# Gated cross-attention block on one core: head weights centred and scaled in place by GpSimd and split by ScalarE, ternary steps spread over three engines, factors and clip on GpSimd, one tile for v and vx

## The chip, the cores and the metric

The kernel runs on one core of one Trainium2 chip. The metric is device time in microseconds (us) from start to end of the execution; lower is better. TensorE (PE), VectorE (DVE), ScalarE (ACT) and GpSimd (POOL) each work through their own queue of instructions in order; SyncE (SP) issues the transfers, also in order. They wait for one another through semaphores.

## The reference, cut to what matters

```python
# x: 4 batches x 512 rows x 512; ctx: the same; 8 groups of heads, 2 query heads each, D = 128
ln  = layernorm(layernorm(x)) * ln_w + ln_b
q, k, v = (e4m3(clip(bf16(ln / in_scale), -448, 448)) * in_scale @ W.T * w_scale for each)
q, k = head_layernorm(q), head_layernorm(k)          # mean and variance over the 128 of a head
core = softmax(q @ k.T / sqrt(D)) @ v
qx   = head_layernorm(fp8_linear(ln, wqx));  kx, vx = split(ctx @ w_kv_x.T)
xout = softmax(qx @ head_layernorm(kx).T / sqrt(D)) @ vx
catq = e4m3(bf16(clip(concat(core, xout) / smooth, -448, 448)))
x    = x + tanh(g0) * (catq @ wproj.T) * proj_scale
# feed-forward: weights are made ternary: clip(round(w / mean|w|), -1, 1); activations 8 bit
x    = x + tanh(g1) * bitlinear(silu(a) * b, w_down),  a, b = split(bitlinear(layernorm(x), w_gate_up))
```

## The kernel before, in words

The attention part runs 32 iterations, one for each of the 4 batches and 8 groups of heads. An iteration has 16 slots, so there are 512 slots of scores, with 28 lead-in slots before the first and 20 after the last. Each engine's program is one loop over the slot number `n`, in which fixed tables say what else is to be issued in a slot (`PREP_HI`, `KV_AT`, `OUT_AT`, `X_AT`, `JOB_AT`); so the order of work on each engine is written out by hand. In every slot VectorE takes the row maximum of the scores (`row_max`), the reciprocal of the sums (`recip`) and the low half of the probabilities (`lo`); ScalarE takes the exponential and the high half; SyncE transposes the probabilities (`turn`); TensorE multiplies them with v some slots later. Numbers that need more than 16 bits are kept as a high and a low float16 half, and both are multiplied.

Work around that stream:

- **Head weights** (`prep_at`, `kv_at`), group by group during the lead-in and iterations 0 to 5, for later batches they are read back from `ws`. Two buffers `raw` take a quarter `kt` of a group's weights (128x768) or the context weights (128x1024). `head_means` (VectorE) takes the mean over each head, `center` (GpSimd) subtracts it, `prep_w` on GpSimd scales four column ranges into the high half, and `prep_w` on VectorE makes four low halves from them. `kv_hi` and `kv_lo` do the same for the context weights. `load_raw` refills a buffer after `w_dn`.
- **Heads**: `stats_a/b` (VectorE) and `rstd_a/b` (GpSimd) in even slots, `norm_a/b` and `v_lo` (VectorE) in odd ones, then transposes by TensorE, `head_y` (ScalarE), `head_hi` and `head_lo` (GpSimd).
- **group_factors** (VectorE), once for each iteration: five small instructions, one after another.
- **Outputs**: for each of two pairs in an iteration `out_step` (VectorE) clips, takes the exponent field, scales it and adds it, and `out_sub` (GpSimd) subtracts.
- **Jobs** (`JOBS`, `job`): from slot 92 to slot 305, 48 sums of the feed-forward weights (ScalarE) and 32 splits of the projection weights (GpSimd, VectorE, ScalarE); from slot 309 to 436, 48 ternary conversions (VectorE). They use the same two `raw` buffers, some six jobs in an iteration.

After the attention part comes the feed-forward part, 16 tiles of 128 rows. The change leaves it alone.

## Time and profile before

| | |
|---|---|
| median of three runs | 2029.97 us (2029.39 to 2035.35) |
| the profiled execution | 2037.14 us |
| its span in the trace | 2035.4 us |
| lead-in, up to the first row maximum | 0 to 138.06 us |
| iterations 0 to 5 | 138.06 to 507.78 us, 61.6 us each |
| iterations 6 to 18 | 507.78 to 1089.16 us, 44.7 us each |
| iterations 19 to 27 | 1089.16 to 1520.29 us, 47.9 us each |
| iterations 28 to 31 and feed-forward | 1520.29 to 2035.4 us |

An iteration's start is the start of its first row maximum on VectorE. Busy time is the time in which an engine executes an instruction; a row of a group gives the operation, the tile written and those read, partitions x elements, the count, busy us and mean ns, and then the engine's idle time just ahead and what ended it.

### The profile page before, as it was taken

The numbers are of one execution on the slowest core, as the hardware profiler recorded it, in microseconds if no ns is written. First come the engines' busy times: TensorE is split into PE (matmuls) and PEld (weight loads), VectorE is DVE, ScalarE is ACT, GpSimd is POOL, SyncE is SP. The second block draws the span as 40 slices with busy tenths as digits, with TensorE's granted clock in tenths as the row PEclk, the third lists the DMA queues.
The fourth block names the chain that finished last, engine by engine and source line by source line (L and its number), as shares of the span: only waits on it lengthen the run. The fifth ranks groups of instructions, "written<-read, shape, count | busy, mean of one in ns | idle before, by whom it ended". The sixth has DMA issues, their size and how long they took to land.

```text
span 2035.4 us, 34986 instructions
## 1 busy us (share of the span) xinstructions
PE 1677.8 (82%) x11147; PEld 1020.8 (50%) x11164; DVE 1747.3 (86%) x4062; ACT 1186.9 (58%) x2963; POOL 1017.2 (50%) x1327
## 2 busy tenths in 40 slices
PE   1467777767999988889998878898999967999996
...
GB/s 85 90 115 143 145 158 137 143 148 166 190 215 197 224 206 202 177 188 214 201 200 187 176 163 181 194 214 212 204 182 154 126 231 225 117 74 103 73 17 16
DMA packets 632027, 325.45 MB, mean 160 GB/s; under 512 B 547744, under 2 KB 590880, under 8 KB 626720
## 3 DMA queue, kind: packets, MB, share of 16 engines
q1 hardware_dynamic: 631840, 323.16, 67.6%
...
## 4 chain that ended last, share of the span: by engine, by line
DVE 44%; PE 28%; DMA 12%; POOL 7%; issue 7%; ACT 2%; SPq 1%; POOLq 0%; DVEq 0%; ACTq 0%
DVE pp L943 8%; DMA pt<-pp 8%; DVE nmx L933 8%; PE psum L682 5%; PE psum L640 4%; PE psum L657 4%; PE psum L628 4%; PE psum L600 4%; PE psum L699 3%; PE psum L607 3%; DMA raw<-in_w 3%; DVE xh L916 2%; DVE wbt L821 2%; POOL raw L1348 2%; DVE ast L902 1%
## 5 line engine op out<-in xcount | busy, mean ns | idle before, releaser
L628 PE MATMUL psum<-qk 128*128 128x512 f16 x1536 | 429.8, 390 | 71.4 <-DVE pp L943 69.3
L600 PE MATMUL psum<-wbt,xqt 128*128 128x256 f16 (+1 forms) x4096 | 421.6, 255 | 50.8 <-DVE xh L916 35.3
L600 PEld LDWEIGHTS psum<-wbt,xqt 128*128 128x128 f16 x4096 | 340.7, 102 | 167.3 <-DVE xh L916 40.1
L1231 ACT ACTIVATE psum<-psum,nmx 128x512 f32<-128x512 f32 x512 | 340.6, 665 | 143.7 <-DVE nmx L933 138.6
L943 DVE SCALAR_TENSOR_TENSOR pp<-psum,prs,pp 128x512 f16<-128x512 f32 x512 | 378.2, 739 | 31.0 <-ACT pp L1242 31.0
L1242 ACT ACTIVATE pp<-psum,prs 128x512 f16<-128x512 f32 x512 | 350.7, 685 | 62.5 <-DMA pt<-pp 62.4
L933 DVE TENSOR_REDUCE nmx<-psum 128x1 f32<-128x512 f32 x512 | 343.4, 671 | 26.9 <-PE psum L628 26.0
L1237 ACT ACTIVATE prs<-psm 128x1 f32<-128x1 f32 x512 | 107.4, 210 | 250.4 <-DVE psm L938 248.5
L640 PE MATMUL psum<-pt,vs 128*128 128x512 f16 x768 | 208.5, 396 | 52.7 <-ACT cy L1250 28.2
L1424 POOL TENSOR_TENSOR qk<-y,qk 128x512 f16<-128x512 f32 x192 | 233.3, 1215 | 16.0
L628 PEld LDWEIGHTS psum<-qk 128*128 128x128 f16 x1536 | 144.3, 100 | 162.7 <-DVE pp L943 74.0
L640 PE MATMUL psum<-pt,vx 128*128 128x512 f16 x768 | 203.6, 389 | 21.4 <-ACT cy L1250 19.6
L607 PE MATMUL psum<-wbt,ctxh 128*128 128x256 f16 x1536 | 199.8, 283 | 1.6 <-DVE ctxh L788 1.5
L1399 POOL TENSOR_TENSOR ars<-ast,eps 128x4 f32<-128x4 f32 x128 | 54.5, 426 | 286.8 <-DVE ast L903 286.7
L607 PEld LDWEIGHTS psum<-wbt,ctxh 128*128 128x128 f16 x1536 | 156.0, 102 | 54.7 <-issue 5.8
L1431 POOL TENSOR_TENSOR cy<-cy,cc 128x512 f16<-128x512 bf16 x128 | 152.6, 1193 | 41.2 <-DVE cy L959 41.2
L617 PE MATMUL psum<-idf,xh 128*128 128x128 f32 x768 | 121.0, 281 | 53.5 <-DVE vx L893 31.8
L1410 POOL TENSOR_TENSOR brs<-bst,eps 128x2 f32<-128x2 f32 x128 | 45.6, 356 | 236.7 <-DVE bst L910 236.1
L1224 ACT ACTIVATE y<-psum,hb,hw 128x512 f32<-128x512 f32 x192 | 151.3, 788 | 8.6 <-PE psum L617 8.6
L640 PEld LDWEIGHTS psum<-pt,vs 128*128 128x128 f16 x768 | 74.3, 100 | 159.4 <-issue 70.2
L1402 POOL TENSOR_TENSOR ars<-ars,mhalf 128x4 f32<-128x4 f32 x128 | 135.8, 1061 | 10.0
L1483 POOL TENSOR_SCALAR frs<-fmv 128x1 f32<-128x1 f32 x16 | 3.0, 191 | 267.4 <-DVE fmv L1013 267.3
...
## 6 DMA issues: line engine op xcount, KB each, us to landing
...
pt<-pp SPq DMA_TRANSPOSE x512, 3.3
...
```

The lines of the kernel that those rows point to most:

```text
L600: ins = e.matmul(bank[:, o0:o0 + c1 - c0], xv[:, v, kt * 512 + tt * 128:kt * 512 + (tt + 1) * 128], wb[i][:, h, kt, c0:c1], start=kt == 0 ...
L607: ins = e.matmul(bank[:, 256:512], ctxh[:, u, kt, ts], wkvb[i][:, w, kt, :], start=kt == 0 and k == 0, stop=kt == 3 and k == 2)
L628: ins = e.matmul(SB(n), qk[i][:, jq, u, ss], qk[i][:, jk, w, :], start=k == 0, stop=k == 2)
L640: ins = e.matmul(OB, v[:, t, u, :], src[:, w, t, :], start=t == 0 and k == 0, stop=t == 3 and k == 2)
L933: e.tensor_reduce(nmx[:, n % 8:n % 8 + 1], SB(n), AX, ALU.max, negate=True).then_inc(s["mx"], 1)
L943: e.scalar_tensor_tensor(pp[k][:, 1, :], SB(n), prs[:, n % 8:n % 8 + 1], pp[k][:, 0, :], ALU.mult, ALU.subtract).then_inc(s["lo"], 1)
L1224: e.activation(y32[n % 2][:], psum[:, BANK["T", n], :], ACT.Identity, bias=hb[:, vec:vec + 1], scale=hw[:, vec:vec + 1]).then_inc(s["y32"], 1)
L1231: e.activation(SB(n), SB(n), ACT.Exp, bias=nmx[:, k], accum_out=psm[:, k]).then_inc(s["exp"], 1)
L1242: e.activation(pp[n % 4][:, 0, :], SB(n), ACT.Copy, scale=prs[:, n % 8:n % 8 + 1]).then_inc(s["hi"], 1)
L1402: e.tensor_tensor(rs[:, 1, :], rs[:, 0, :], mhalf[:, 0:4], ALU.pow).then_inc(s["a_rs"], 1)
L1424: e.tensor_tensor(qk[it % 2][:, j, 1, :], y32[n % 2][:], qk[it % 2][:, j, 0, :], ALU.subtract).then_inc(s["hd_lo"], 1)
L1431: e.tensor_tensor(y.bitcast(F16), y, tmp, ALU.subtract).then_inc(s["o_q"], 1)
```

## The change

1. **Head weights.** GpSimd's `prep_scale` centres and scales each head in place in `raw` by one instruction with two factors (five of 128x128, and a sixth for v without a mean). ScalarE's `prep_hi` copies the 128x768 into the high half, VectorE's `prep_lo` makes the low half by one subtraction. `kv_scale`, `kv_hi`, `kv_lo` are the same for the context weights. The slots of the steps move (`PREP_AT`, `KV_AT`); the chain has one more engine in it.
2. **Ternary.** GpSimd scales and takes the lower of it and 1, VectorE takes the higher of it and -1 and adds the rounding constant, ScalarE takes it off again and writes bfloat16. Each is one slot after the other.
3. **Splits.** The subtraction moves from VectorE to GpSimd.
4. **group_factors and the clip** of the outputs move to GpSimd; the later steps of an output move back by one slot, its store too.
5. **v and vx** get one scale and one tile `vv`: one instruction of 128x256 in `v_hi` and in `v_lo` instead of two of 128x128.
6. `load_raw` of the next group's second quarter is issued ahead of `store_w` instead of behind it; in the lead-in two `head_means` stand earlier.

```diff
-PREP_HI = (-10, -6, -4, -1)
-KV_AT = {"part": 2, "spread": 3, "whole": 4, "fac": 5, "hi": 5, "lo": 6}
-OUT_AT = {"clip": 17, "field": 18, "step": 19, "add": 20, "sub": (21, 23), "store": 26}
+PREP_AT = (-9, -5, -3, 1)
+KV_AT = {"part": 2, "spread": 3, "whole": 4, "fac": 5, "scaled": 5, "hi": 6, "lo": 7}
+OUT_AT = {"clip": 17, "field": 19, "step": 20, "add": 21, "sub": (22, 24), "store": 27}
...
-            def prep_w(it, kt):
+            def prep_lo(it, kt):
                 k, i = it * 5 + kt, it % 2
-                r = raw[k % 2]
-                for c0, c1, v in COLS:
-                    q.wait_ge("w_hi", (it * 4 + kt) * 4 + v + 1)
-                    ins = e.scalar_tensor_tensor(wb[i][:, 1, kt, c0:c1], r[:, c0:c1], ratio[:, v, kt:kt + 1],
-                                                 wb[i][:, 0, kt, c0:c1], ALU.mult, ALU.subtract)
-                ins.then_inc(s["w_dn"], 1)
+                q.wait_ge("w_hi", it * 4 + kt + 1)
+                e.tensor_tensor(wb[i][:, 1, kt, :], raw[k % 2][:, 0:768], wb[i][:, 0, kt, :],
+                                ALU.subtract).then_inc(s["w_dn"], 1)
...
+            def ternary(m):
+                if JOBS[m][0] == "tern":
+                    f = raw[(K0 + m) % 2][:, 0:512]
+                    q.wait_ge("l_t0", JV["l_t2", m])
+                    e.tensor_scalar(f, f, -1.0, MAGIC, ALU.max, ALU.add).then_inc(s["l_t1"], 1)
...
+            def prep_hi(it, kt):
+                k, i = it * 5 + kt, it % 2
+                q.wait_ge("wc", it * 4 + kt + 1)
+                q.wait_ge("gb", (it - 1) * 4)
+                q.wait_ge(f"w_st{i}", 16 * (it // 2))
+                e.activation(wb[i][:, 0, kt, :], raw[k % 2][:, 0:768], ACT.Copy).then_inc(s["w_hi"], 1)
...
+            def prep_scale(it, kt):
+
+                k = it * 5 + kt
                 r = raw[k % 2]
+                q.wait_ge("wm", k + 1)
                 q.wait_ge("const_ready", 1)
+                for h, (c, v) in enumerate(HEAD_COLS):
+                    e.tensor_scalar(r[:, c:c + 128], r[:, c:c + 128], wmean[:, k % 2, h:h + 1], ratio[:, v, kt:kt + 1],
+                                    ALU.subtract, ALU.mult)
...
+            def out_clip(pair):
+                y = cy[pair % 3][:]
+                q.wait_ge("o_y", 2 * pair + 2)
+                e.tensor_scalar(y, y, 448.0, -448.0, ALU.min, ALU.max).then_inc(s["o_c"], 1)
```

On VectorE, in an iteration that prepares weights, a quarter's low half stood as four instructions behind the output step, directly ahead of the next quarter's means:

```order
L957 TENSOR_SCALAR cc<-cc 128x1024
L821 SCALAR_TENSOR_TENSOR wbt<-raw,ratio,wbt 128x256 x2
L821 SCALAR_TENSOR_TENSOR wbt<-raw,ratio,wbt 128x128 x2
L813 TENSOR_REDUCE wmean<-raw 128x5
L814 TENSOR_SCALAR wmean<-wmean 128x5
```

After the change, the same place for the first quarter of a group; `wmean` now belongs to a slot of its own:

```order
L896 TENSOR_TENSOR xh<-psum,ars 128x512
L804 TENSOR_TENSOR wbt<-raw,wbt 128x768
L918 RECIPROCAL psm<-psm 128x1
L913 TENSOR_REDUCE nmx<-psum 128x1
L923 SCALAR_TENSOR_TENSOR pp<-psum,prs,pp 128x512
L890 BN_STATS bst<-psum 128x6
L798 TENSOR_REDUCE wmean<-raw 128x5
```

Four instructions became one, and the low half is two slots behind the scaling instead of one.

On GpSimd before, one quarter between the output subtraction and the next `rstd_a`:

```order
L1348 TENSOR_TENSOR raw<-raw,wmean 128x640
L1367 TENSOR_SCALAR wbt<-raw,ratio 128x256 x2
L1367 TENSOR_SCALAR wbt<-raw,ratio 128x128 x2
L1399 TENSOR_TENSOR ars<-ast,eps_0 128x4
L1402 TENSOR_TENSOR ars<-ars,mhalf 128x4
```

and after, in the fullest slot, where a head, the clip and a quarter stand behind one another ahead of the next `rstd_b`:

```order
L1416 TENSOR_TENSOR qk<-y_1,qk 128x512
L1447 TENSOR_SCALAR cy<-cy 128x1024
L1355 TENSOR_SCALAR raw<-raw,wmean,ratio 128x128 x5
L1357 TENSOR_SCALAR raw<-raw,ratio 128x128
L1402 TENSOR_TENSOR brs<-bst,eps_1 128x2
L1404 TENSOR_TENSOR brs<-brs,mhalf 128x2
```

Five instructions of a quarter became six, and the clip stands ahead of them. On SyncE before, the refill of `raw` behind the store of a whole group (`ws`):

```order
L395 DMA_TRANSPOSE pt<-pp 128x8x128 x6
L383 DMA ws<-wbt 128x8192
L379 DMA raw<-in_w 128x768
L395 DMA_TRANSPOSE pt<-pp 128x8x128
L379 DMA raw<-in_w 128x768
```

and after:

```order
L377 DMA raw<-in_w 128x768
L393 DMA_TRANSPOSE pt<-pp 128x8x128
L381 DMA ws<-wbt 128x8192
L393 DMA_TRANSPOSE pt<-pp 128x8x128
L377 DMA raw<-in_w 128x768
```

The first refill moved ahead of the store, with one transpose between them.

## Rows read from the trace of the kernel before

**Rows 1.** The page, part 1: busy time, share, instructions.

```profile
PE 1677.8 (82%) x11147; PEld 1020.8 (50%) x11164; DVE 1747.3 (86%) x4062; ACT 1186.9 (58%) x2963; POOL 1017.2 (50%) x1327
```

**Rows 2.** Windows: the stages of the kernel, busy us by engine.

```profile
core 0: us, PE busy (x) PEld busy (x) DVE busy (x) ACT busy (x) POOL busy (x), PEclk, DMA share, GB/s
0.00:138.06 138.06, 48.65 (x312) 35.96 (x313) 90.76 (x235) 17.51 (x33) 68.71 (x110) 0.74 0.27 93
138.06:507.78 369.72, 272.10 (x1785) 171.59 (x1784) 323.16 (x753) 202.62 (x506) 237.43 (x320) 0.90 0.63 148
507.78:1089.16 581.38, 531.03 (x3880) 348.45 (x3878) 553.02 (x1281) 465.63 (x1247) 374.92 (x472) 0.99 0.89 201
1089.16:1520.29 431.13, 373.92 (x2675) 238.90 (x2673) 414.08 (x1006) 293.03 (x749) 239.22 (x294) 0.98 0.85 190
1520.29:2035.40 515.11, 452.10 (x2504) 225.92 (x2519) 366.26 (x795) 208.12 (x430) 96.94 (x135) 0.95 0.46 114
```

**Rows 3.** Windows, columns as before: iterations 29, 9, 8 and 20.

```profile
1563.28:1602.42 39.14, 39.14 (x298) 26.53 (x297) 37.02 (x89) 31.09 (x81) 23.89 (x32) 1.00 0.62 122
641.68:682.80 41.12, 38.93 (x292) 25.71 (x291) 39.55 (x94) 36.07 (x98) 27.23 (x35) 1.00 0.89 207
596.31:641.68 45.37, 41.52 (x311) 27.51 (x309) 43.31 (x103) 35.08 (x95) 31.13 (x43) 1.00 1.02 224
1139.76:1193.38 53.62, 42.38 (x303) 26.25 (x301) 53.10 (x131) 32.55 (x82) 27.01 (x32) 1.00 0.80 175
```

**Rows 4.** Groups by form: the head weights on VectorE and GpSimd.

```profile
L821 DVE SCALAR_TENSOR_TENSOR wbt<-raw,ratio,wbt 128x256 f16<-128x256 f32 x64 | 37.8, 629 | 35.2 <-POOL wbt L1367 35.2
L821 DVE SCALAR_TENSOR_TENSOR wbt<-raw,ratio,wbt 128x128 f16<-128x128 f32 x64 | 28.0, 475 | 0.0
L837 DVE SCALAR_TENSOR_TENSOR wbt<-raw,wfa,wbt 128x1024 f16<-128x1024 f32 x8 | 10.2, 1275 | 3.2 <-POOL wbt L1376 3.2
L1348 POOL TENSOR_TENSOR raw<-raw,wmean 128x640 f32<-128x640 f32 x32 | 40.9, 1277 | 16.2 <-DVE wmean L814 16.2
L1367 POOL TENSOR_SCALAR wbt<-raw,ratio 128x128 f16<-128x128 f32 x64 | 32.8, 523 | 0.0
L1367 POOL TENSOR_SCALAR wbt<-raw,ratio 128x256 f16<-128x256 f32 x64 | 30.0, 479 | 3.2
L1259 ACT ACTIVATE raw<-raw 128x512 f32<-128x512 f32 x48 | 31.1, 647 | 0.0
```

**Rows 5.** Waits: VectorE for a refill of `raw`.

```profile
DVE wmean L813 <- DMA raw<-in_w: 7.5, 6, 2.8
```

**Rows 6.** Groups by form: clip, split, ternary, v on VectorE.

```profile
L952 DVE TENSOR_SCALAR cy<-cy 128x1024 bf16<-128x1024 bf16 x64 | 30.7, 480 | 11.9 <-ACT cy L1250 11.9
L984 DVE TENSOR_TENSOR raw<-raw,wps 128x512 f16<-128x512 f32 x32 | 30.2, 943 | 0.0
L976 DVE TENSOR_SCALAR raw<-raw,wsc 128x512 f32<-128x512 f32 x48 | 23.9, 497 | 0.3 <-DMA raw<-in_wgu 0.3
L977 DVE TENSOR_SCALAR raw<-raw 128x512 bf16<-128x512 f32 x48 | 21.1, 439 | 1.6
L978 DVE TENSOR_SCALAR raw<-raw 128x512 bf16<-128x512 bf16 x48 | 15.8, 329 | 1.7
```

**Rows 7.** Windows of the instructions that touch `kfac`: VectorE, then ScalarE.

```profile
0.00:2035.40 2035.40, 52.47 (x160) 45.01 (x64) 0.94 0.68 160
```

**Rows 8.** Groups by form: long elementwise work on GpSimd.

```profile
L1376 POOL TENSOR_SCALAR wbt<-raw,wfa 128x1024 f16<-128x1024 f32 x8 | 8.9, 1118 | 0.8
L1424 POOL TENSOR_TENSOR qk<-y,qk 128x512 f16<-128x512 f32 x192 | 233.3, 1215 | 16.0
L1418 POOL TENSOR_SCALAR qk<-y 128x512 f16<-128x512 f32 x192 | 119.3, 621 | 32.6 <-ACT y L1224 31.0
```

**Rows 9.** Source lines on VectorE: ns min/median/max, first and last start.

```profile
L957 DVE TENSOR_SCALAR cc<-cc x64: 407/976/1332, 210.5 to 1701.3; 128x1024 bf16<-128x1024 bf16 x64
L955 DVE TENSOR_SCALAR cc<-cy x64: 398/408/819, 206.2 to 1700.9; 128x1024 uint16<-128x1024 uint16 x64
```

More of the change, by code:

```diff
@@ L288, in flamingo @@
         qk = [a(f"qk{i}", [128, 6, 2, 512], F16) for i in range(2)]
-        vs = [a(f"vs{i}", [128, 4, 2, 128], F16) for i in range(3)]
-        vx = [a(f"vx{i}", [128, 4, 2, 128], F16) for i in range(3)]
+        vv = [a(f"vv{i}", [128, 4, 2, 2, 128], F16) for i in range(3)]
         pp = [a(f"pp{i}", [128, 2, 512], F16) for i in range(4)]
@@ L637, in pv @@
                     q.wait_ge("o_y", hc)
-                src, v = pt[hc % 2], vx[it % 3] if att else vs[it % 3]
+                src, v = pt[hc % 2], vv[it % 3]
                 for k, (u, w) in enumerate(((0, 0), (0, 1), (1, 0))):
-                    ins = e.matmul(OB, v[:, t, u, :], src[:, w, t, :], start=t == 0 and k == 0, stop=t == 3 and k == 2)
+                    ins = e.matmul(OB, v[:, t, u, att, :], src[:, w, t, :], start=t == 0 and k == 0, stop=t == 3 and k == 2)
                 if t == 3:
@@ L1078, in dve_program @@
             ins.then_inc(s["pre_h"], 1)
+            head_means(0, 0)
+            head_means(0, 1)
             for t in range(4):
@@ L1099, in dve_program @@
             e.tensor_tensor(hr2[:, 2:4], hf[:, 2:4], hm2[:, 0:2], ALU.mult).then_inc(s["pre_r"], 1)
-            for kt in range(4):
-                head_means(0, kt)
-                prep_w(0, kt)
+            prep_lo(0, 0)
+            head_means(0, 2)
+            prep_lo(0, 1)
+            head_means(0, 3)
             for col, v in ((0, 0), (1, 0), (2, 1), (3, 1), (4, 2)):
@@ L1144, in dve_program @@
                         stats_b(it, tt)
-                for k, step in enumerate(("clip", "field", "step", "add")):
+                for k, step in enumerate(("field", "step", "add")):
                     for pair in pairs_at(n, OUT_AT[step]):
                         out_step(pair, k)
-                for it, kt in prep_at(n - 1):
-                    prep_w(it, kt)
+                for it, kt in prep_at(n - 2):
+                    prep_lo(it, kt)
                 for it, kt in prep_at(n + 1):
@@ L1259, in job @@
                     e.activation(f, f, ACT.Abs, accum_out=wsum[:, col:col + 1]).then_inc(s["l_sum"], 1)
+                elif what == "tern":
+                    q.wait_ge("l_t1", JV["l_t2", m])
+                    q.wait_ge(f"l_st{i}", JV[f"l_st{i}", JB[m][0]])
+                    e.activation(o.bitcast(BF16)[:, 0:512], f, ACT.Identity, bias=magic[:, 0:1]).then_inc(s["l_t2"], 1)
                 elif what == "split":
@@ L1268, in act_program @@
                     x_turned(0, kt, v)
+                prep_hi(0, v)
+            kv_hi(0)
             q.wait_ge("pre_w", 1)
@@ L1283, in act_program @@
                     head_y(it, o)
+                for it, kt in prep_at(n - 1):
+                    prep_hi(it, kt)
+                for it in kv_at(n, "hi"):
+                    kv_hi(it)
                 for b, kt in x_steps(n, "turn"):
@@ L1446, in pool_program @@
             for kt in range(4):
-                prep_w(0, kt)
+                prep_scale(0, kt)
             w_spread(0)
             c_spread(0)
-            kv_hi(0)
+            kv_scale(0)
             for kt in range(4):
                 ctx_hi(0, kt)
+            group_factors(0)
             for n in range(FIRST, PAST):
+                ph, j = divmod(n, SLOTS)
+                if j == FACTORS_AT and 0 < ph + 2 < NIT:
+                    group_factors(ph + 2)
                 for it, tt, half in tiles_at(n - 1):
@@ L1461, in pool_program @@
                     head_lo(it, o)
+                for pair in pairs_at(n, OUT_AT["clip"]):
+                    out_clip(pair)
                 for k in range(2):
@@ L1465, in pool_program @@
                 for it, kt in prep_at(n):
-                    prep_w(it, kt)
+                    prep_scale(it, kt)
                 for it in kv_at(n, "spread"):
                     w_spread(it)
-                for it in kv_at(n, "hi"):
-                    kv_hi(it)
+                for it in kv_at(n, "scaled"):
+                    kv_scale(it)
                 for b, _ in x_steps(n, "rstd"):
```

166 lines of the change are left out of this document (71 added, 95 removed).

## Prediction

> **What bounds the kernel now.** I read the page's busy shares first: VectorE is busy 86% of the span, TensorE 82%, ScalarE 58%, GpSimd 50% [rows 1]. That is a mean over stages with different limits, so the windows by stage come next; the reader should compare, in each, busy VectorE and busy TensorE with the length [rows 2].
>
> - Iterations 0 to 5: 369.7 us, VectorE 323.2 (87%), TensorE 272.1 (74%, at a granted clock of 0.90), GpSimd 237.4. TensorE has room; VectorE and what it waits for set the pace. By the groups its idle time is largely a wait for GpSimd's scaled weights: 35.2 us ahead of the low halves over the whole kernel [rows 4], and 7.5 us ahead of the means, for a refill of `raw` [rows 5].
> - Iterations 6 to 18: 581.4 us, VectorE 553.0 (95%), TensorE 531.0 (91%). Iterations 19 to 27: 431.1 us, VectorE 414.1 (96%), TensorE 373.9. VectorE is the fuller one, but another limit stands close by: iteration 29, without weights and jobs, takes 39.14 us, and TensorE is busy in all of them at full clock; iteration 9 with jobs takes 41.12; iteration 8 takes 45.37 with the transfer engines busy for all of it (share 1.02) [rows 3]. So 39.1 us is TensorE's floor for an iteration, and some iterations are held by transfers.
> - The rest, 515 us, holds four short iterations and the feed-forward part, where the change has almost nothing.
>
> **The sum, part by part.** It is made against the profiled execution's own 2037.1 us (span 2035.4); the median of the three runs is 7.2 us lower, and I carry that over at the end.
>
> *Head weights.* VectorE spends 37.8 + 28.0 busy and 35.2 waiting on 32 quarters, 3.16 us each [rows 4]. A 128x768 subtraction with two inputs is not in the trace. From below, the 128x512 of the split at 0.94 [rows 6], from above the 128x1024 low half at 1.28 [rows 4]; midway, 1.1. That is 2.05 us less for each quarter, if ScalarE's copy is ready two slots after the scaling. Eleven of the quarters lie in the lead-in, 21 in iterations 0 to 5. GpSimd did 1.28 + 2 x 0.52 + 2 x 0.48 = 3.3 us for a quarter [rows 4]; its six 128x128 instructions are 3.1 at that row's 0.52 (the two-factor form isn't shown; it could cost 4.0 if each were half as long again). ScalarE gets a copy of 128x768: 0.65 for 512 [rows 4], so 0.97, and it has 45% of its time free there [rows 2]. The context weights change by nothing much: one low half of 1.28 stays one.
>
> *Refill.* It stood behind a 2 MB store, now ahead of it, and every refill has two slots: the 7.5 us [rows 5] go, nearly all in iterations 0 to 5. If the slots shrink too far, they stay.
>
> *Clip and factors.* VectorE loses 30.7 us of clips [rows 6] and 52.5 us of instructions on `kfac` [rows 7], together 83.2, or 2.6 us in each of 32 iterations. GpSimd gets two clips of 128x1024, 1.12 each by its nearest row [rows 8], and four tiny ones; 3 us an iteration. The joined v instruction I count as nothing: two neighbours of 128x128 overlap.
>
> *Splits.* 30.2 us leave VectorE [rows 6], all in iterations 6 to 18; GpSimd's subtraction of that size takes 1.2 [rows 8], 32 times 39 us on a GpSimd that is busy 374.9 of 581.4.
>
> *Ternary.* Three instructions, 60.8 us and 3.6 between them [rows 6], become one like the first, 23.9: 40.5 us off VectorE. GpSimd and ScalarE each get 0.6 us six times an iteration [rows 4, 8]; they have room.
>
> Now by stage:
>
> 1. Lead-in: 11 x 2.05 = 23, and little else. VectorE waits there for GpSimd's `rstd` in any case, a refill takes longer than two short slots, and the first `head_means` now stand ahead of the x statistics. I keep 15.
> 2. Iterations 0 to 5: 21 x 2.05 = 43, 7.5 of refills, 6 x 2.6 = 16; 66 in all. The new chain passes through three in-order queues: while ScalarE waits for `prep_scale`, the next exponential is queued behind it, and VectorE's reciprocal waits for that. In the fullest slot GpSimd has a head (1.84), a clip (1.12) and a quarter (3.1) to do, 6 us where a slot is 3. I take 0.6 us for each of 21 quarters, 13 us. 66 - 13 = 53: 51 to 52 us for a plain iteration. If that chain fits, all 66 come; if each quarter waits 2 us, only 24.
> 3. Iterations 6 to 18: VectorE's 553.0 fall by 34 and 30 to 489, 37.6 an iteration, under TensorE's 39.1. From there TensorE and the transfers set the time: 39.1, the 2.0 by which iteration 9 exceeds it, and 1.7 for iterations that transfers hold (8, 16) or that also prepare the next x: 42.8, times 13 = 556. That is 25 less, not 64.
> 4. Iterations 19 to 27: VectorE's 414.1 fall by 23 and 40.5 to 350. Iteration 20 is the fullest, 53.62 with VectorE at 53.10 [rows 3]; it and its two neighbours come down by some 7 us each, the six others by 2.3 each until TensorE and transfers hold them near 42.5. That is 35.
> 5. Iterations 28 to 31: already at the floor; 1. Feed-forward: nothing.
>
> Sum: 15 + 53 + 25 + 35 + 1 = 129; 2037.1 - 129 = 1908 for such an execution, and 7 less for the median: **1901 us**.
>
> **A rule against it.** The row of the step instruction has a minimum of 407 ns and a median of 976, that of the exponent field, of the same size, a median of 408 [rows 9]: the same kind of work takes 0.57 us longer where it meets something, and that slot is the one in which GpSimd does a head.
> The Trainium skill (SBUF — State Buffer, Who interferes with whom) says that VectorE in a two-port mode or with two inputs from SBUF and GpSimd hold one shared pair of ports exclusively, so that whoever comes second stands still; the trace agrees with it in those two rows. By that rule more GpSimd work makes VectorE's remaining steps longer; by a reading without it the steps keep their mean.
> By the rule the sum is that of the first rival, 1946; by the rows with their mean unchanged it is 1901.
>
> **The rivals.**
>
> *VectorE and GpSimd get in each other's way.* GpSimd goes from 39.6 us an iteration to 43 of 52 (iterations 0 to 5), and from 28.8 to 35 of 42.8 (6 to 18): 29 + 2 clips 2.2 + factors 0.8 + 2.5 splits 3.0. Each iteration has six output steps on VectorE; two already pay 0.57. If the other four do as well, that is 2.3 us an iteration, 73 over 32; about 1 us of it an iteration hides in TensorE's lead in the later stages, so 45 remain: 1946. For it: the 0.57. Against: the field stood behind the statistics without a delay, and GpSimd pays when it comes second. Chance 0.15.
>
> *TensorE and transfers hold everything from iteration 6 on.* For it: iteration 29 at 100% TensorE, and the transfer share of 0.89 and 0.85 in both stages. Then only lead-in and iterations 0 to 5 gain, and 10 us of the rest: 2030 - 68 - 10 = 1952. Against: iterations 20 to 22 are 53 us with TensorE at 42. Chance 0.12.
>
> *All that leaves VectorE pays.* Lead-in 23, iterations 0 to 5 66, 6 to 18 down to 40.1 each, 60, iterations 19 to 27 50, 2 at the end: 201, 1829. It needs transfers to stretch no further and GpSimd never late. Chance 0.15.
>
> *Slower: GpSimd's queue delays `rstd`.* There are 256 `rstd`, each due one slot after its statistics, and VectorE stands still for a late one; behind it `norm`, and TensorE's bank behind that. New work ahead of them in the queue is 1.1 to 3 us at a time. It decides from 129 / 256 = 0.5 us of added delay for each; at 0.6 the time is 1901 + 154 = 2055. Against: `rstd` stands first in its slot, and GpSimd is not above 85% in any stage. Chance 0.05.
>
> **How the numbers follow.** My forecast (1875 to 1925) has 0.50; the rivals 0.15, 0.12, 0.15, 0.05, and 0.03 is left for mixtures beyond them. The bounds of single costs move it: new waits per quarter 0 to 2 us (+13 to -29), the 128x768 at 0.94 or 1.28 (5 us either way), two-factor instructions at 4.0 a quarter (some 10 us more). From 1848 to 1948 the range takes in the forecast, the first rival, half of the second and a third of the third. Within 0.3% (6 us) a measurement can't tell this kernel's time from no change: faster 0.94, same 0.01, slower 0.05.
>
> **What would show it in the profile after.** Iterations 0 to 5 at 50 to 53 us, no wait of VectorE on scaled weights, and the low half at 0.95 to 1.3 us; iterations 6 to 18 near 42.8 with VectorE's share below TensorE's; iterations 20 to 22 at 46 to 47; the first row maximum near 123 us. Wrong it is if the step, field and add rows on VectorE grow by half a microsecond (first rival), if VectorE waits for `ars` and `brs` come to over 100 us (the slower one), if stages after slot 96 don't move (second), or if GpSimd's clip costs twice 1.12.

## The result: 1.4% slower, and the profile after

| | us, median (lowest to highest) |
|---|---|
| before, timed beside the change | 2032.66 (2029.39 to 2036.19) |
| after | 2059.98 (2057.23 to 2066.28) |
| ratio | 1.0138, 95% interval 1.0107 to 1.017 |
| profiled execution of after | 2066.28, span 2064.5 |

Forecast were 1901 us and a range of 1848 to 1948. The page's part 1 of the kernel after, to set beside [rows 1]:

```profile
PE 1692.5 (82%) x11147; PEld 1028.2 (50%) x11164; DVE 1592.2 (77%) x3487; ACT 1228.9 (60%) x2923; POOL 1301.7 (63%) x1655
```

VectorE lost 155 us of work, TensorE did the same matmuls, and the time rose: what left VectorE was not paid back. GpSimd gained 284 us, more than left VectorE. Part 4 of the page, the chain that ended last, names the new pacemaker. First before, then after:

```profile
DVE 44%; PE 28%; DMA 12%; POOL 7%; issue 7%; ACT 2%; SPq 1%; POOLq 0%; DVEq 0%; ACTq 0%
...
POOL 35%; PE 27%; DVE 20%; DMA 8%; issue 5%; ACT 4%; SPq 1%; POOLq 0%; DVEq 0%; ACTq 0%
```

GpSimd's share went from 7% to 35%. The windows by stage, bounds by the same slots as [rows 2] (columns as there: lead-in's own row is left out):

```profile
145.32:511.33 366.01, 276.98 (x1770) 171.47 (x1769) 296.90 (x627) 219.87 (x509) 299.11 (x391) 0.87 0.63 151
511.33:1109.15 597.82, 540.63 (x3881) 354.36 (x3880) 505.72 (x1104) 459.55 (x1194) 435.07 (x579) 0.97 0.87 196
1109.15:1546.24 437.09, 374.99 (x2675) 240.42 (x2673) 350.91 (x809) 313.30 (x762) 358.64 (x398) 0.98 0.85 188
```

In the next table the first column is a length in us, the others are differences from it; e7 is the fastest of the experiments below.

| stage | before | forecast | after | best variant (e7) |
|---|---|---|---|---|
| lead-in | 138.1 | -15 | +7.3 | -4.5 |
| iterations 0 to 5 | 369.7 | -53 | -3.7 | -38.7 |
| 6 to 18 | 581.4 | -25 | +16.4 | +2.4 |
| 19 to 27 | 431.1 | -35 | +6.0 | -24.5 |
| rest | 515.1 | -1 | +3.2 | -3.6 |

VectorE is busy for 81%, 85% and 80% of the three stages; no engine is over 91% in any of them, so waits must hold the kernel. Groups by form of the kernel after show two surprises and two confirmations:

```profile
L1355 POOL TENSOR_SCALAR raw<-raw,wmean,ratio 128x128 f32<-128x128 f32 x160 | 135.4, 857 | 3.9 <-DVE wmean L799 3.8
L1433 POOL TENSOR_SCALAR raw<-raw,wsc 128x512 f32<-128x512 f32 x48 | 100.1, 2086 | 1.3 <-DMA raw<-in_wgu 0.4
L1447 POOL TENSOR_SCALAR cy<-cy 128x1024 bf16<-128x1024 bf16 x64 | 70.3, 1098 | 25.9 <-ACT cy L1228 20.5
L804 DVE TENSOR_TENSOR wbt<-raw,wbt 128x768 f16<-128x768 f32 x32 | 38.3, 1196 | 6.3 <-ACT wbt L1187 6.3
L896 DVE TENSOR_TENSOR xh<-psum,ars 128x512 f32<-128x512 f32 x128 | 87.5, 684 | 67.0 <-POOL ars L1394 66.1
L905 DVE TENSOR_TENSOR xh<-psum,brs 128x256 f32<-128x256 f32 x128 | 53.5, 418 | 68.0 <-POOL brs L1404 68.0
L944 DVE TENSOR_SCALAR raw<-raw 128x512 f32<-128x512 f32 x48 | 23.6, 493 | 57.4 <-POOL raw L1433 57.4
```

The clip (1098 ns against 1120) and the 128x768 low half (1.20 us against 1.1) cost what was forecast. Centring and scaling of 128x128 costs 857 ns where 520 were taken, a quarter 5 x 0.857 + 0.425 = 4.7 us instead of 3.1; the ternary's first step costs 2.09 us where 0.6 were taken, 48 times. Two waits of VectorE come with it: 57.4 us for GpSimd's step of the ternary conversion, and 66.1 + 68.0 = 134 us for the two `rstd`, 35.0 of it in the lead-in, 52.6 in iterations 0 to 5 and 35.0 in 6 to 18. Before, the two `rstd` cost 14.3 (who waited for whom, us in total, times, longest):

```profile
DVE xh L916 <- POOL ars L1402: 9.6, 9, 1.4
DVE xh L925 <- POOL brs L1412: 4.7, 8, 1.2
```

How such a wait comes about, in the timeline of GpSimd and VectorE in the kernel after, in iteration 17 (start, duration, engine; in brackets the idle time before):

```profile
1027.12 0.43 DVE L890 BATCH_NORM_STATS2 bst<-psum 128x6 f32<-128x256 f32 x1 [0.40 <-PE psum L606]
...
1027.67 1.04 POOL L1447 TENSOR_SCALAR cy<-cy 128x1024 bf16<-128x1024 bf16 x1
...
1028.79 0.62 POOL L1437 TENSOR_SCALAR wps<-raw 128x512 f16<-128x512 f32 x1
...
1029.49 1.16 POOL L1442 TENSOR_TENSOR raw<-raw,wps 128x512 f16<-128x512 f32 x1
...
1030.61 0.19 POOL L1402 TENSOR_TENSOR brs<-bst,eps 128x2 f32<-128x2 f32 x1
...
1030.88 0.71 POOL L1404 TENSOR_TENSOR brs<-brs,mhalf 128x2 f32<-128x2 f32 x1
...
1031.68 0.42 DVE L905 TENSOR_TENSOR xh<-psum,brs 128x256 f32<-128x256 f32 x1 [2.13 <-POOL brs L1404]
```

The statistics are ready at 1027.55. GpSimd takes them up at 1030.61, because the clip, the high half and the moved subtraction of the split (L1447, L1437, L1442) stand in front. VectorE stands for 2.13 us. That `rstd` is first in its slot doesn't help: the slot before is still being worked off.

### The profile page after: what moved, and what is told of

Same layout as the page of the kernel before. It is cut to its first block, busy times and chain, and to the rows that moved or that the text cites. A ratio compares the mean times of both kernels' runs of the same rounds, so it can differ in the third digit from the quotient of the medians.

```text
span 2064.5 us, 34605 instructions
## 1 busy us (share of the span) xinstructions
PE 1692.5 (82%) x11147; PEld 1028.2 (50%) x11164; DVE 1592.2 (77%) x3487; ACT 1228.9 (60%) x2923; POOL 1301.7 (63%) x1655
## 4 chain that ended last, share of the span: by engine, by line
POOL 35%; PE 27%; DVE 20%; DMA 8%; issue 5%; ACT 4%; SPq 1%; POOLq 0%; DVEq 0%; ACTq 0%
DMA pt<-pp 8%; POOL raw L1355 6%; PE psum L681 5%; POOL qk L1416 5%; PE psum L656 5%; DVE pp L923 4%; POOL raw L1433 4%; DVE nmx L913 4%; PE psum L639 4%; PE psum L627 3%; PE psum L599 3%; POOL cy L1423 3%; POOL brs L1404 3%; PE psum L698 3%; POOL ars L1394 3%
## 5 line engine op out<-in xcount | busy, mean ns | idle before, releaser
L627 PE MATMUL psum<-qk 128*128 128x512 f16 x1536 | 438.1, 396 | 47.2 <-DVE pp L923 46.4
L639 PE MATMUL psum<-pt,vv 128*128 128x512 f16 x1536 | 414.2, 394 | 70.6 <-ACT cy L1228 37.2
L599 PE MATMUL psum<-wbt,xqt 128*128 128x256 f16 (+1 forms) x4096 | 426.0, 256 | 49.7 <-DVE xh L896 34.6
L639 PEld LDWEIGHTS psum<-pt,vv 128*128 128x128 f16 x1536 | 151.2, 101 | 276.5 <-issue 98.2
L1416 POOL TENSOR_TENSOR qk<-y,qk 128x512 f16<-128x512 f32 x192 | 240.1, 1250 | 16.0
L606 PEld LDWEIGHTS psum<-wbt,ctxh 128*128 128x128 f16 x1536 | 154.1, 101 | 60.8 <-DVE ctxh L787 12.1
L1423 POOL TENSOR_TENSOR cy<-cy,cc 128x512 f16<-128x512 bf16 x128 | 147.6, 1154 | 19.4 <-DVE cy L937 19.4
L1394 POOL TENSOR_TENSOR ars<-ars,mhalf 128x4 f32<-128x4 f32 x128 | 134.9, 1054 | 10.0
L1410 POOL TENSOR_SCALAR qk<-y 128x512 f16<-128x512 f32 x192 | 125.9, 656 | 24.0 <-ACT y L1202 18.3
L896 DVE TENSOR_TENSOR xh<-psum,ars 128x512 f32<-128x512 f32 x128 | 87.5, 684 | 67.0 <-POOL ars L1394 66.1
L1355 POOL TENSOR_SCALAR raw<-raw,wmean,ratio 128x128 f32<-128x128 f32 x160 | 135.4, 857 | 3.9 <-DVE wmean L799 3.8
```

The lines of the kernel that those rows point to most:

```text
L599: ins = e.matmul(bank[:, o0:o0 + c1 - c0], xv[:, v, kt * 512 + tt * 128:kt * 512 + (tt + 1) * 128], wb[i][:, h, kt, c0:c1], start=kt == 0 ...
L606: ins = e.matmul(bank[:, 256:512], ctxh[:, u, kt, ts], wkvb[i][:, w, kt, :], start=kt == 0 and k == 0, stop=kt == 3 and k == 2)
L627: ins = e.matmul(SB(n), qk[i][:, jq, u, ss], qk[i][:, jk, w, :], start=k == 0, stop=k == 2)
L639: ins = e.matmul(OB, v[:, t, u, att, :], src[:, w, t, :], start=t == 0 and k == 0, stop=t == 3 and k == 2)
L1355: e.tensor_scalar(r[:, c:c + 128], r[:, c:c + 128], wmean[:, k % 2, h:h + 1], ratio[:, v, kt:kt + 1], ALU.subtract, ALU.mult)
L1394: e.tensor_tensor(rs[:, 1, :], rs[:, 0, :], mhalf[:, 0:4], ALU.pow).then_inc(s["a_rs"], 1)
```

## Experiments

The stages of each run, in us; bounds by the same slots. Ratios are to the kernel before, run beside it, with 95% intervals; "before" and "after" have their numbers in the section above.

| run | time, ratio | lead-in | 0 to 5 | 6 to 18 | 19 to 27 | rest |
|---|---|---|---|---|---|---|
| before | | 138.1 | 369.7 | 581.4 | 431.1 | 515.1 |
| after | 1.0138 | 145.3 | 366.0 | 597.8 | 437.1 | 518.3 |
| e1 | 2022.82, 0.993 [0.9908, 0.9952] | 134.9 | 333.1 | 600.1 | 437.7 | 516.5 |
| e2 | 2056.4, 1.0092 [1.0065, 1.012] | 146.3 | 366.0 | 600.3 | 427.0 | 517.3 |
| e3 | 2071.83, 1.0174 [1.0133, 1.0214] | 145.4 | 368.8 | 594.4 | 447.9 | 518.9 |
| e4 | 1995.82, 0.9778 [0.9733, 0.9823] | 134.8 | 333.9 | 600.1 | 412.4 | 511.8 |
| e5 | 1991.73, 0.9766 [0.9742, 0.9791] | 134.8 | 334.0 | 605.1 | 401.4 | 518.4 |
| e6 | 1983.0, 0.9736 [0.9713, 0.9759] | 134.3 | 332.8 | 597.2 | 402.4 | 512.9 |
| e7 | 1970.25, 0.9678 [0.9651, 0.9705] | 133.6 | 331.0 | 583.7 | 406.6 | 511.5 |
| e8 | 1973.38, 0.9688 [0.9652, 0.9725] | 134.6 | 333.6 | 591.0 | 404.6 | 515.8 |
| e9 | 1987.28, 0.9771 [0.9739, 0.9803] | 133.6 | 331.7 | 597.4 | 403.3 | 517.7 |
| e10 | 1976.15, 0.9705 [0.9667, 0.9743] | 133.0 | 341.8 | 578.8 | 411.8 | 515.7 |
| e11 | 2005.57, 0.9876 [0.9832, 0.992] | 137.9 | 358.2 | 577.7 | 416.1 | 507.0 |
| e12 | 2143.56, 1.0553 [1.0533, 1.0573] | 137.9 | 361.8 | 571.8 | 425.6 | 645.8 |
| e13 | 2096.67, 1.0321 [1.0301, 1.0341] | 138.0 | 352.2 | 550.0 | 409.7 | 645.5 |

The stages of a run are read from one profiled execution, and several executions of one kernel differ by up to 17 us. Where two kernels have the same code in a stage, it can be seen how well a length repeats: iterations 6 to 18 are the same in after, e1, e2 and e4, and took 597.8, 600.1, 600.3 and 600.1 us; iterations 19 to 27 are the same in e4 and e5, apart from one last split, and took 412.4 and 401.4. So a difference of 2 to 3 us between two stages means nothing in what follows, and in 19 to 27 one of ten can be chance.

### What does an instruction cost on GpSimd? (m1, a micro kernel)

GpSimd alone runs twelve forms of the same instruction, three times each, with no work on the other engines meanwhile.

> Twelve forms of GpSimd's tensor_scalar by themselves, 128x512 float32 (two of them 128x128), three times each, nothing beside them; x is only copied to the output, the rest of the computation is left out. Theory A (the pair of operations sets the price, whatever runs beside it): multiply by a pointer and multiply by 1.0 takes 0.6 us, multiply and minimum about 2.1, subtract and multiply about 2.4 to 2.8, subtract and multiply on 128x128 0.8. Theory B (the long times in the changed kernel come from VectorE at the shared ports): all forms of one size take 0.6 us here, those of 128x128 0.4.

The source lines of that kernel (ns minimum, median, maximum): L40 multiplies by a pointer operand and by 1.0; L41 multiplies by a pointer and takes a minimum; L42 is the same with immediates (numbers written in the instruction); L43 takes minimum and maximum by immediates, L44 both by pointer; L45 subtracts and multiplies by pointers, L46 by immediates; L47 multiplies twice by pointers; L48 multiplies and adds, L51 with immediates; L49 and L50 are L45 and L40 at 128x128.

```profile
L40 POOL TENSOR_SCALAR z<-t,p x3: 686/686/687, 3.4 to 32.1; 128x512 f32<-128x512 f32 x3
L41 POOL TENSOR_SCALAR z<-t,p x3: 2002/2002/2010, 4.2 to 32.9; 128x512 f32<-128x512 f32 x3
L42 POOL TENSOR_SCALAR z<-t x3: 1917/1917/1918, 6.3 to 35.0; 128x512 f32<-128x512 f32 x3
L43 POOL TENSOR_SCALAR z<-t x3: 612/612/613, 8.3 to 37.0; 128x512 f32<-128x512 f32 x3
L44 POOL TENSOR_SCALAR z<-t,p x3: 757/757/757, 9.0 to 37.7; 128x512 f32<-128x512 f32 x3
L45 POOL TENSOR_SCALAR z<-t,p x3: 2076/2076/2077, 9.9 to 38.6; 128x512 f32<-128x512 f32 x3
L46 POOL TENSOR_SCALAR z<-t x3: 1922/1922/1922, 12.1 to 40.8; 128x512 f32<-128x512 f32 x3
L47 POOL TENSOR_SCALAR z<-t,p x3: 767/767/767, 14.1 to 42.8; 128x512 f32<-128x512 f32 x3
L48 POOL TENSOR_SCALAR z<-t,p x3: 687/687/687, 14.9 to 43.7; 128x512 f32<-128x512 f32 x3
L49 POOL TENSOR_SCALAR z<-t,p x3: 792/792/792, 15.7 to 44.4; 128x128 f32<-128x128 f32 x3
L50 POOL TENSOR_SCALAR z<-t,p x3: 367/367/368, 16.6 to 45.3; 128x128 f32<-128x128 f32 x3
L51 POOL TENSOR_SCALAR z<-t x3: 617/617/617, 17.1 to 45.8; 128x512 f32<-128x512 f32 x3
```

Size, types and layout of the 128x512 forms are equal, and the cost is 0.61 to 0.77 us or 1.9 to 2.1 us. A pointer in place of an immediate costs 0.07 to 0.09, two of them 0.15. What decides is the pair of operations: multiply-multiply, multiply-add and minimum-maximum are cheap, multiply-minimum and subtract-multiply dear. Nothing ran beside it, so neighbours and ports are no part of that; in the kernel the two dear forms are another 8% and 4% longer (857 against 792 ns, 2086 against 2002). Subtract-multiply is a little cheaper here than the 2.4 to 2.8 that were expected.

### The cheap forms in the kernel (e1, e4), and the ternary back on VectorE (e2)

e1 replaces the five subtract-multiply pieces of a quarter, and the four of the context weights, by one centring and multiply-multiply pieces, in place:

```diff
-                for h, (c, v) in enumerate(HEAD_COLS):
-                    e.tensor_scalar(r[:, c:c + 128], r[:, c:c + 128], wmean[:, k % 2, h:h + 1], ratio[:, v, kt:kt + 1],
-                                    ALU.subtract, ALU.mult)
+                q.done(e.tensor_tensor(cols, cols, wmean[:, k % 2, 0:5].unsqueeze(2).broadcast_to([128, 5, 128]),
+                                       ALU.subtract))
+                for c0, c1, v in COLS:
+                    ins = e.tensor_scalar(r[:, c0:c1], r[:, c0:c1], ratio[:, v, kt:kt + 1], 1.0, ALU.mult, ALU.mult)
```

> The changed kernel, but the head weights are centred by one tensor_tensor and scaled by four instructions that multiply twice, in place, as the kernel before did them (3.3 us a quarter by its rows instead of 4.7). Theory A (the form of the six instructions costs the gain in iterations 0 to 5): these iterations come down from 61.0 us to 54 to 57, the first row maximum from 145 to 138 or less, the total by 25 to 45 us, to 2015 to 2035. Theory Q (the place in GpSimd's queue matters, not the form): less than 10 us.

e4 adds that the ternary clips before it scales: GpSimd takes minimum and maximum with the mean and its negative, VectorE multiplies by the reciprocal and adds the rounding constant.

```diff
-                    e.tensor_scalar(f, f, wsc[:, k:k + 1], 1.0, ALU.mult, ALU.min).then_inc(s["l_t0"], 1)
+                    e.tensor_scalar(f, f, wsc[:, k - 2:k - 1], wsc[:, k - 4:k - 3], ALU.min, ALU.max).then_inc(s["l_t0"], 1)
...
-                    e.tensor_scalar(f, f, -1.0, MAGIC, ALU.max, ALU.add).then_inc(s["l_t1"], 1)
+                    e.tensor_scalar(f, f, wsc[:, k:k + 1], MAGIC, ALU.mult, ALU.add).then_inc(s["l_t1"], 1)
```

> The changed kernel with all its work on the same engines, but in forms that were short by themselves: the head weights as in the earlier run (centre by one tensor_tensor, then multiply twice), and the ternary step as minimum and maximum against plus and minus the mean on GpSimd, multiply and add on VectorE, add on ScalarE. Theory A (the slow forms are all that went wrong): 1960 to 1990, iterations 23 to 26 at 43, iterations 6 to 18 below 581. Theory A+Q (forms cost stages 0 to 5 and 19 to 27, the queue costs 6 to 18): 2000 to 2015, with iterations 6 to 18 still at 595 to 600 and 23 to 26 at 43 to 44.5.

Groups of e4, the same work as L1355 and L1433 of after:

```profile
L1358 POOL TENSOR_TENSOR raw<-raw,wmean 128x640 f32<-128x640 f32 x32 | 42.9, 1340 | 12.0 <-DVE wmean L800 11.9
L1361 POOL TENSOR_SCALAR raw<-raw,ratio 128x256 f32<-128x256 f32 x64 | 35.8, 571 | 3.2
L1361 POOL TENSOR_SCALAR raw<-raw,ratio 128x128 f32<-128x128 f32 x64 | 24.6, 396 | 0.0
L1435 POOL TENSOR_SCALAR raw<-raw,wsc 128x512 f32<-128x512 f32 x48 | 40.0, 833 | 4.7 <-DMA raw<-in_wgu 3.8 <-DMA raw<-in_wd 0.8
```

A quarter falls to 1.34 + 2 x 0.57 + 2 x 0.40 = 3.3 us, near the 3.1 of the sum, and a ternary step to 0.83. Where these stand the time falls: e1 takes 10 us from the lead-in and 33 from iterations 0 to 5 and nothing elsewhere; e4 takes 25 more from 19 to 27. Together they turn +1.4% into -2.2%; from after to e4 the span is 71.5 us shorter. e1 came as theory A said. e4 came between its two theories (1995.82), with iterations 6 to 18 still at 600 as the second said.

e2 is after with the ternary's three steps on VectorE, as before.

> The changed kernel, but the ternary conversion is VectorE's alone again, three instructions as before. Theory A (GpSimd's multiply-and-minimum of 2.09 us makes VectorE stand, 57 us in all): iterations 23 to 26 come from 46.9 us to 44 to 45, the total falls by 10 to 20 us. If the three-engine version is worth having, the total rises instead by up to 20.

Iterations 23 to 26 fall from 46.9 to 43.6 us each and the stage by 10 to 427.0, less than by e4's 25. The whole fell by less than the 10 to 20 us expected: 1.0092 against 1.0138, with overlapping intervals. So moving the ternary off VectorE was probably worth it, but only in the cheap form.

### Who delays `rstd` in iterations 6 to 18? (e3, e5 to e10)

With cheap forms these iterations still take 600 us; nothing dear runs there. e3 is after with the clip one slot later: `OUT_AT = {"clip": 18, ...}` instead of 17.

> The changed kernel with one number changed: GpSimd's clip stands one slot later, in an even slot behind rstd, not in the odd slot behind a head. No work is added or taken away. Theory Q (rstd is late because head, clip and job stand ahead of it in GpSimd's queue): VectorE's waits for rstd in iterations 6 to 18 (35 us) fall by half or more and these iterations by 8 to 20 us in all, iterations 0 to 5 by 5 to 15. Theory A alone: no change in iterations 6 to 18.

The wait for `brs` fell from 68.0 to 37.9 over the kernel, but VectorE's exponent field, now close behind the clip, waited 66.2 us for it:

```profile
DVE cc L933 <- POOL cy L1447: 66.2, 49, 14.0
DVE xh L896 <- POOL ars L1394: 64.7, 30, 5.5
DVE xh L905 <- POOL brs L1404: 37.9, 26, 6.0
```

In iterations 6 to 18 the waits for `rstd` fell from 35.0 to 20.2 us, and the one for the clip put 25.1 in their place; the stage fell by 3.4 us where theory Q had 8 to 20, and iterations 0 to 5 didn't fall at all. The wait changed its name: a new place in the queue is not enough. The next runs take work off the queue, on top of e4: e5 returns the split's subtraction to VectorE, e6 the clip, e8 both, e9 the factors alone, e7 all three. Each moves back the lines of the diff for that part, for example for e6:

```diff
+                for pair in pairs_at(n, OUT_AT["clip"]):
+                    y = cy[pair % 3][:]
+                    q.wait_ge("o_y", 2 * pair + 2)
+                    e.tensor_scalar(y, y, 448.0, -448.0, ALU.min, ALU.max).then_inc(s["o_c"], 1)
```

> As e4, and the split's subtraction is VectorE's again. If GpSimd's queue costs iterations 6 to 18 (head, clip and split stand ahead of rstd in one slot), these fall by 8 to 20 us against e4, though VectorE gets 30 us more to do; if VectorE's load sets them, they rise by up to 20. No other stage moves.

> As e4, and the clip is VectorE's again, in the same slot. By the queue theory the waits for rstd fall in all stages and the total by 10 to 25 us; iterations 6 to 18 by 5 to 15. If VectorE's load sets the time, nothing or up to 10 us more.

> As e4, with split, clip and factors all on VectorE again; what stays of the change is the head weights by three engines, the ternary step by three engines, one tile for v and vx, the later output slots and the refill ahead of the store. By the queue theory iterations 6 to 18 come to 575 to 582 as in the kernel before and VectorE's wait for rstd to under 20 us; the total 1975 to 2000. If VectorE's load sets the time it is slower than e4 by 10 to 30.

> The changed kernel with the cheap head-weight and ternary forms, with the split's subtraction and the clip back on VectorE, and the factors of a group still on GpSimd. Its 6 to 18 were 597.8 us in the changed kernel, 605.1 with the split alone back, 597.2 with the clip alone back and 583.7 with split, clip and factors back. Theory A (GpSimd's queue ahead of rstd, and the two large pieces are what is long in it): with both gone the factors' four instructions (1.45 us an iteration) are too short to matter; its 6 to 18 are 583 to 588, VectorE's waits for rstd under 6 us in them, the time 1970 to 1976. Theory B (the factors in their slot are what meets rstd): its 6 to 18 stay at 594 or above, the waits for rstd stay above 8 us, the time is 1980 to 1990.

> The changed kernel with the cheap forms, and the factors of a group back on VectorE; split subtraction and clip stay on GpSimd. Theory A (split and clip make the queue long): its 6 to 18 stay at 594 to 602, the waits for rstd above 20 us, the time 1988 to 1998. Theory B (the factors are what meets rstd): its 6 to 18 fall to 583 to 590, the waits for rstd below 12 us, the time 1975 to 1985.

In iterations 6 to 18, waits of VectorE for `ars` and `brs` together, and the stage: after 35.0 and 597.8; e4 35.0 and 600.1; e5 8.5 and 605.1; e6 17.4 and 597.2; e9 27.9 and 597.4; e8 under 6 and 591.0; e7 about 1 and 583.7. Against e4 no single part brings more than 3 us, which is within the spread, the two large ones 9, all three 16.4. e9 came as its theory A said (its time 1 us under that range), and so did e8 but for the stage, 3 us over: split and clip together are what is long in the queue. e7 came as the queue theory said to within 2 us of its stage and of its waits, with a total 5 us under the range. That the factors add the last 7 us isn't shown: e7 and e8 differ by 0.1% in time (0.9678 and 0.9688), and e8's profiled execution was 8 us above its median. e5 and e6 missed what the queue theory forecast for this stage (8 to 20 and 5 to 15 us), and e6's total fell in 19 to 27 instead. The waits for `rstd` alone don't give the length either: e5 cuts them to a quarter and gains nothing, as VectorE has 15.6 us more work and waits 15.7 us for the split's high half. TensorE slows too: from before to after its busy time there grows from 531.0 to 540.6 us while its granted clock falls from 0.99 to 0.97 (0.95 to 0.97 in e1 to e6, e8 and e9), and in e7 both are back. Whether the lower clock lengthens the stage or only follows from TensorE's longer pauses, no run separates:

```profile
464.59:1048.33 583.74, 531.01 (x3889) 347.48 (x3887) 546.55 (x1227) 462.65 (x1195) 364.69 (x472) 0.99 0.88 201
```

e10 puts e7's output steps back into their old slots, each one earlier.

> As the kernel with cheap forms and split, clip and factors back on VectorE (its 6 to 18: 583.7 us, time 1970.3), and the steps of an output pair back in the slots that they had before the change (field 18, step 19, add 20, sub 21 and 23, store 26: each one earlier). Theory A (TensorE and the transfers hold its 6 to 18, and the slots of these steps are indifferent): its 6 to 18 are 581 to 586, the time 1966 to 1974. Theory B (the later slots of the steps cost what VectorE's shorter work should have given): its 6 to 18 fall to 572 to 579, the time is 1958 to 1966.

Stage 6 to 18 goes to 578.8, as theory B said, but iterations 0 to 5 to 341.8, 11 us longer, and the time, 1976.15, is in neither range; the two kernels' intervals overlap. The later slots cost nothing on balance.

### Why iterations 6 to 18 never gain (e11 to e13)

Even e7, with 6.5 us less work on VectorE, is no shorter there than before. So the last runs start from the kernel before. e11 relieves VectorE and loads nobody: clip, multiplication and addition of an output pair work on 8 of 1024 columns.

```diff
-                    ins = e.tensor_scalar(y, y, 448.0, -448.0, ALU.min, ALU.max)
+                    ins = e.tensor_scalar(y[:, 0:8], y[:, 0:8], 448.0, -448.0, ALU.min, ALU.max)
```

> The kernel before, with the clip, the multiplication and the addition of an output pair done on 8 of the 1024 columns, so the output lacks that rounding: VectorE is relieved of some 1.6 us a pair, two pairs an iteration, about 43 us in its 6 to 18 (26 pairs at 414, 847 and 670 ns, less some 60 to 100 ns each that a tiny one takes), and nothing is put on another engine. Theory A (beside VectorE, TensorE with its gaps and the transfers of the probabilities hold an iteration in its 6 to 18, so relief of VectorE could not have paid there whatever GpSimd did): its 6 to 18 fall by less than 10 us, to 571 or more, and the waits for the transfers of pt grow by 10 us or more. Theory B (VectorE, busy for 95% there, was the bound, and the changed kernel lost its relief to GpSimd's queue alone): its 6 to 18 fall by 25 to 43 us, to 538 to 556. As in the forecast (its 6 to 18 limited by TensorE's 39.1 us of busy time and some 3.7 of gaps): a fall of 20 to 27 us, to 554 to 561.

e12 thins transfers instead, e13 does both:

```diff
-                e.dma_start(wbt[:, it % 2, :], ws[it % NG]).then_inc(s[f"w_ld{it % 2}"], 16)
+                e.dma_start(wbt[:, it % 2, 0:2048], ws[it % NG][:, 0:2048]).then_inc(s[f"w_ld{it % 2}"], 16)
...
-                e.dma_start(raw[k % 2][:, 0:512], late_src[src][:, j, :]).then_inc(s[f"raw_ld{k % 2}"], 16)
+                e.dma_start(raw[k % 2][:, 0:128], late_src[src][:, j, 0:128]).then_inc(s[f"raw_ld{k % 2}"], 16)
```

> The kernel before with thinner transfers: from iteration 6 on an iteration loads a quarter of its weights (0.5 MB instead of 2 MB; the rest are the weights that the buffer held), and a job loads 128 of its 512 columns; the output is computed from those. No engine's work changes. The kernel before spends 581.4 us in its 6 to 18. Theory A (three limits lie within some 5 us an iteration: VectorE in iterations 12 to 14, TensorE and the transfers of the probabilities, queued behind the weights and the jobs, in the others): its 6 to 18 fall by 3 to 12 us, and the waits of TensorE and ScalarE for pt<-pp (19.2 and 18.5 us) fall below 20 together. Theory B (transfers don't limit): its 6 to 18 within 3 us of 581.

> As the kernel with the clip, multiplication and addition of an output pair on 8 columns (its 6 to 18: 577.7 us, the waits for pt<-pp 21.9 and 21.6), and the transfers thinned as well (a quarter of the weights from iteration 6 on, a quarter of each job's load). Theory A (the transfers are what held that kernel when VectorE was relieved): its 6 to 18 fall to 550 to 568, near the 13 x 42.8 = 556 of the forecast or below, with TensorE busy for 94% or more and the waits for pt<-pp under 20 us together. Theory B (something else than VectorE and transfers holds them: TensorE itself, its clock, ScalarE): its 6 to 18 stay at 573 or more.

Windows of iterations 6 to 18: e11, e12, e13 (before is in [rows 2]):

```profile
496.11:1073.86 577.75, 531.88 (x3880) 350.68 (x3878) 529.66 (x1279) 464.21 (x1247) 361.88 (x472) 0.98 0.89 203
...
499.63:1071.45 571.82, 530.44 (x3873) 345.93 (x3874) 552.69 (x1280) 464.79 (x1247) 371.86 (x471) 0.99 0.70 142
...
490.22:1040.24 550.02, 522.50 (x3882) 345.78 (x3880) 526.92 (x1281) 462.59 (x1247) 359.86 (x471) 1.00 0.75 148
```

| iterations 6 to 18 | transfers full | transfers thin |
|---|---|---|
| VectorE full | 581.4 | 571.8 |
| VectorE relieved by 23 to 26 us | 577.7 | 550.0 |

Relief is worth 3.6 us with full transfers and 21.8 with thin ones; thinning is worth 9.6 and 27.7. Both e12 and e13 came as their theory A said, e13 with TensorE busy for 95%. In e11 the waits for `pt<-pp` of TensorE and ScalarE come to 43.5 us (before, 37.7: they grew by 5.8 us where theory A had 10 or more); in e12 and e13 they are 0.5 and 1.2. By iteration, 12 to 14, the ones in which VectorE is busiest, gain 6.1 us in e11, and 7, 9 and 11 lose as much. In the stages around it e11's relief pays nearly in full: 11.5 us in iterations 0 to 5 for 10.7 us of work, 15.0 in 19 to 27 for 16.9; some of that is the execution, the fastest of e11's four, 6.7 us under their median. (Relief was 23 us of busy time in e11 and 26 from e12 to e13 where 43 were written, since the multiplication of 8 columns still takes 573 ns. The rest of e12 and e13 is longer by 130 us: TensorE runs 3033 matmuls there instead of 2504, since the kernel has a branch for weights whose low part counts, and their data take it. Only the stages up to iteration 27 are read from them.)

## Why the prediction was wrong, step by step

1. *"GpSimd's six 128x128 instructions are 3.1 at that row's 0.52"* and *"GpSimd and ScalarE each get 0.6 us six times an iteration."* Wrong, the first cause. I priced an operation by size and types from rows of another pair of operations. Measured 4.7 us a quarter, over my upper bound of 4.0, and 2.09 us a ternary step, for which I gave no bound. The bound was also wrongly reckoned: six instructions of 0.52, each half as long again, are 4.7 and not 4.0, which is what came. m1 shows the cause, e1 and e4 its worth: 71.5 us of span.
2. *Iterations 0 to 5, "I take 0.6 us for each of 21 quarters, 13 us."* The path that I charged was that of ScalarE, whose wait for `prep_scale` holds up an exponential and with it VectorE's reciprocal. ScalarE did wait, 58.8 us in this stage, but VectorE's reciprocal waited 0.2 us for it. What cost was `rstd`, for which my sum had nothing: 52.6 us of waits (before, 0.5). With 66 us to gain, 13 would be left; measured were 3.7. The waits in this stage, after:

```profile
ACT wbt L1187 <- POOL raw L1357: 58.8, 20, 5.5
DVE psm L918 <- ACT psum L1209: 0.2, 1, 0.2
```

With cheap forms (e4) the `rstd` waits are 19.6 and the stage gains 35.8; in e7 they are 2.4 and it gains 38.7. But e7 has clip and factors back on VectorE, for which the 66 held 16; without them my sum would have said 66 - 16 - 13 = 37, so its part on head weights and refills came about right once the forms were cheap. The 16 of clip and factors did not come. The windows of this stage, e4 and e7:

```profile
134.80:468.72 333.92, 261.27 (x1763) 164.67 (x1761) 299.71 (x628) 218.91 (x509) 258.48 (x352) 0.92 0.70 165
...
133.59:464.59 331.00, 262.68 (x1763) 165.78 (x1761) 310.82 (x668) 219.54 (x509) 236.95 (x318) 0.92 0.71 167
```

e4's VectorE has 11.1 us less to do than e7's, its `rstd` waits are 17.2 us longer, and the stage is no shorter. The 128x768 low half is a small term: 1.23 us in this stage in after and 1.13 in e7 instead of 1.1, 3 and 1 us.

3. *Iterations 6 to 18, "From there TensorE and the transfers set the time: 42.8."* Wrong twice. The floor was there with thin transfers: e13 runs 550.0 / 13 = 42.3. With the real ones it is 577.7 / 13 = 44.4 (e11): the first 23 us of relief brought 4, since iterations that transfers hold give back what VectorE's iterations gain. (The sum had 64 us of relief there, of which VectorE's busy time shows 47 in after; how much more than e11's 23 would bring without a load on GpSimd, no run shows.) And the moved work made the stage 16 us longer than before, which e7 takes away. The share of 0.89 in [rows 2] and iteration 8's 1.02 in [rows 3] were signs of it; I put only two of thirteen iterations down to transfers.
4. *Iterations 19 to 27, -35.* The relief of VectorE does pay there (e11). With the cheap form 18.7 us come (e4), in e5 to e9, which have the same ternary steps, 24.5 to 29.7, not far from the forecast. (e5's 29.7 isn't the split's doing: no split lies in this stage.) The dear form ate it all and 6 more: VectorE waited 57.4 us for GpSimd's ternary step, in e4 18.3.
5. *Lead-in, -15.* Dear forms cost 10.5 of the 22 by which it missed (e4). I had kept 8 of 23 us back for two waits of VectorE, and they grew by far more: that for `rstd` from 12.1 us to 35.0 (e7 18.5), and that for a refill of `raw` from 0.7 to 14.4 (e7 16.6). In iterations 0 to 5 the refill's wait did go, as forecast (6.8 to none). No run tests what the lead-in's refills would give; e7 has -4.5.

The rivals. *"GpSimd's queue delays `rstd`"*, at 0.05, is what happened in kind: 134 us of waits, over the 100 that I had named as its sign. That its 2055 us for 0.6 us each stands next to the measured 2060 is partly luck: 134 - 14 = 120 us were added, 0.47 for each of 256, and 1901 + 120 = 2021 by its rule. The other 39 are in the ternary step's wait and in what steps 3 and 5 had missed. What I held against it was that `rstd` is first in its slot and GpSimd below 85%. Neither bears on an in-order queue that is late by one piece: GpSimd is busy 82% of iterations 0 to 5, and the delay comes from the previous slot. *"TensorE and transfers hold everything from iteration 6"*, at 0.12, was right for 6 to 18, as far as e11's relief goes, and wrong for 19 to 27. *"VectorE and GpSimd get in each other's way"* didn't decide. The three steps on VectorE took 413 + 858 + 672 = 1943 ns before and 791 + 409 + 779 = 1979 after:

```profile
L933 DVE TENSOR_SCALAR cc<-cy 128x1024 uint16<-128x1024 uint16 x64 | 50.6, 791 | 13.1 <-POOL cy L1447 13.1
L937 DVE TENSOR_TENSOR cy<-cy,cc 128x1024 bf16<-128x1024 bf16 x64 | 49.9, 779 | 0.1
L935 DVE TENSOR_SCALAR cc<-cc 128x1024 bf16<-128x1024 bf16 x64 | 26.2, 409 | 0.1
```

The step lost its 0.45 us of delay when it moved a slot, the field got 0.38: the stretch goes by the place, and its sum hardly changed. A little further on in the timeline shown above, a field of 1.35 us began 0.09 us after a GpSimd instruction with two inputs and ended 0.28 us after it, where 0.41 is its usual time ([rows 9]):

```profile
1032.27 1.16 POOL L1416 TENSOR_TENSOR qk<-y,qk 128x512 f16<-128x512 f32 x1
1032.36 1.35 DVE L933 TENSOR_SCALAR cc<-cy 128x1024 uint16<-128x1024 uint16 x1
```

The Trainium skill (SBUF — State Buffer, Who interferes with whom) says that VectorE in a two-port mode and GpSimd hold one shared pair of ports exclusively, and that the later one is blocked for the whole instruction. The 1.35 us agree with it; no run here takes the neighbour away.
